# A macaron block (feed-forward, attention, feed-forward): VectorE's small operations in another order, transposes in other PSUM banks, zero filling by GpSimd

## The chip, the core and the metric

The kernel runs on one core of a Trainium2 chip. A core has five engines with a queue each: TensorE (PE), VectorE (DVE), ScalarE (ACT), GpSimd (POOL) and SyncE (SP), the last used for DMA. They run on their own and wait for each other by semaphores. The metric is the device time of one execution in microseconds. Before the change it is 1791.26 us, the median of three runs (1790.68 to 1792.49).

## The reference

```
x = x + 0.5 * ffn(layernorm(x))
x = x + attention(layernorm(x))
x = x + 0.5 * ffn(layernorm(x))

def ffn(x):                       # x: 4 batches x 1024 tokens x 128
    weights = routing(x)          # tokens x 8 experts
    gate = x @ Wg[e];  up = x @ Wu[e]          # 8 experts, 128 x 128 each
    h = silu(gate) * up
    return sum over e of weights[:, e] * (h @ Wd[e])

def routing(x):                   # per token, over the 8 experts
    inh = sigmoid(x @ Wr / temperature)
    w = exp(-|inh - 1/e| / 0.1) where inh lies in a zone, else 0
    where no expert is in the zone: the two best of exp(-|inh - 1/e| / 0.3), normalized
    return w / sum(w)
```

The attention has 16 heads of 64 with rotary positions and its own layernorm with scale and bias; the change does not touch it. Input and output are float32 arrays of 4096 x 128.

## The kernel before

The program is three blocks one after the other: `ffn("f1")`, the attention, `ffn("f2")`. The names f1 and f2 stand for the two feed-forwards below.

A feed-forward makes four turns, t = 0 to 3, one for each batch of 1024 tokens. A turn has 16 units, k = 0 to 15: units 0 to 7 are the eight experts on the first 512 tokens, units 8 to 15 the same experts on the other 512. The running number of a unit is i = 16 t + k. The work of one unit goes through the engines in this order:

- PE, `gate_up` (L481 to L483 twice): three f16 products of 128x512 for the gate into PSUM bank 0 or 1, then three for up into bank 2 or 3. The banks alternate from unit to unit.
- ACT, `silu` (L574): the gate bank to `gate`.
- POOL (L623): `gate` times the token's routing weight, which a DMA has spread over the partitions (`w_all`, a ring of 4), to `gw`.
- DVE (L754): `gw` times the up bank to `hw`. This is called the product of a unit here.
- PE, `down` (L497): four float32 products that add the unit to y in bank 6 (units 0 to 7) or bank 7 (units 8 to 15).
- DVE, `add_y` (L706): y times 0.5 is added to x, once for each bank and turn.

PE's queue in a turn is gate_up(k + 2), down(k), gate_up(k + 3), down(k + 1) and so on. So PE is two units ahead with gate and up. The up products of unit k + 2 wait for the product of unit k (`s_hw`), because they take the same PSUM bank; POOL's L623 of unit k + 2 waits for it too, because it takes the same half of `gw`.

Between the units of a turn the next batch is made ready:

- `norm` on DVE (L283 to L307): the layernorm's mean and inverse root for batch t + 2, 27 small steps, most of them on 128x8 elements, each waiting for the one before it. Its last step (L307) releases ACT's `normed` (L545) at units 0 and 1 of the next turn.
- `transpose` on PE (L448), two halves; `hi` on ACT (L550) and `lo` on DVE (L638) split the result into two f16 parts.
- `router` on PE (L457, 24 small products), `logits` on DVE (L642), `tanh_z` and `tanh_dist` on ACT (L554 to L564), and then `route` on DVE (L664 to L698), 28 parts of which 26 are operations on 128x64 or 128x8 elements.
- `weight_rows` on PE (L470) and `rows` on ACT (L568): the routing weights transposed, then out to memory and back by SP's DMAs as the rows that POOL reads.
- In f1 only: a second `norm`, of 43 steps, for the attention's layernorm of batch t - 1, and POOL's and ACT's `up_low` and `up_high` (L228, L223).

The order of DVE's queue is written out by hand in `turn(t, last)`: the lists `between[k]` and `after_[k]` say which steps stand before and behind the product of unit k. In the last turn of f1 DVE also fills areas for the attention (`clear`, L328 and L334: nine fills of 128x1024 elements and four of 1x1024).

Of the kernel before, what the change touches and what calls it, by code (L numbers as in the profile page):

```python
# [60 lines left out]
def build(nc, x, wg, wu, wd, wr, temp, wdq, wdkv, wup_in, wuv, wo, lns, lnb, rope, out):  # L61
    with ExitStack() as ctx:
# [297 lines left out]
        def ffn(name):  # L360
# [36 lines left out]
            with nc.Block() as block:  # L397
# [41 lines left out]
                def _(pe):  # L439
                    def transpose(p, a):  # L440
# [4 lines left out]
                        elif p > 0:  # L445
                            pe.wait_ge(s_y, 2 * p - 1)
                        for j in range(4):
                            last = nc.tensor.transpose(ps[:, 7, P * j:P * j + P], xn[:, a, j, :], ident[:])  # L448
                        last.then_inc(s_xT, 1)

                    def router(p):

                        pe.wait_ge(s_xlo, 2 * p + 2)
                        for j in range(TB):
                            cols = bass.ds(p * S + P * j, P)
                            for k, (a, b) in enumerate(((xt_hi, wr_hi), (xt_hi, wr_lo), (xt_lo, wr_hi))):
                                last = nc.tensor.matmul(ps[:, 7, E * j:E * j + E], a[:, cols], b[:],  # L457
# [43 lines left out]
                    def turn(t, last):  # L501
                        for k in range(16):
# [32 lines left out]
                def _(act):  # L535
# [12 lines left out]
                    def hi(p, a):  # L548
                        act.wait_ge(s_xT, 2 * p + (a + 1))
                        nc.scalar.copy(xt_hi[:, bass.ds(p * S + 512 * a, 512)], ps[:, 7, :]).then_inc(s_xhi, 1)  # L550
# [15 lines left out]
                    def rows(p, a):  # L566
                        act.wait_ge(s_wr, 2 * p + (a + 1))
                        nc.scalar.copy(w_rows[0:E, p % 2, a, :], ps[0:E, 6, :]).then_inc(s_wt, 1)  # L568
# [7 lines left out]
                    def turn(t, last):  # L576
                        for k in range(16):
# [37 lines left out]
                def _(pool):  # L615
# [11 lines left out]
                    if first:  # L627
                        identities(pool)
                    if first:
# [679 lines left out]
```

## Time and profile before

| | |
|---|---|
| time, median of 3 | 1791.26 us (1790.68 to 1792.49) |
| time of the profiled execution | 1791.68 us |
| its span | 1789.9 us |
| PE busy | 1652.9 us, 92% |
| DVE busy | 1508.4 us, 84% |
| ACT busy | 1238.2 us, 69% |
| POOL busy | 1316.2 us, 74% |
| TensorE clock granted, mean | 0.973 of full speed |
| f1, first to last add_y | 46.2 to 217.7 us |
| f2, to its last add_y | 1786.5 us |

The span is the time from the first to the last instruction that the profiler recorded. Busy shares are averages over three blocks with different limits, so what a change in a feed-forward is worth is read inside f1 and f2. In a timeline, each row is one instruction or some alike behind one another; the number in brackets at its end is how long the engine stood idle before it, and for whom. The duration of an instruction that waits for a resource, and not for a semaphore, contains that wait.

### The profile page before, as it was taken

To read this page: it belongs to the slowest core of one execution; us is meant where nothing else is said; L and a number is where in the kernel's file an instruction comes from. 1 tells how busy PE (TensorE), PEld (TensorE's weight loads), DVE (VectorE), ACT (ScalarE), POOL (GpSimd) and SP (SyncE) were. 2 spreads that over 40 slices of the span, in tenths; PEclk is the share of its full clock that TensorE was granted. 3 is DMA by queue.
4 is the path that set the end of the run, shared out by engine and by line. 5 is a ranking of instruction groups with operands and counts; after the bars stand their busy time and mean duration, and the time that the engine had idled before them with its cause. 6 is when DMAs were issued, how large, how long until landed. Compare 5 with 4: busy or idle time off the path is not lost. (4 is left out here: it accounts for less than half of the span.)

```text
span 1789.9 us, 48884 instructions
## 1 busy us (share of the span) xinstructions
PE 1652.9 (92%) x19376; PEld 1062.1 (59%) x19376; DVE 1508.4 (84%) x3091; ACT 1238.2 (69%) x1747; POOL 1316.2 (74%) x922
## 2 busy tenths in 40 slices
PE   3999766999999999999999999999999999966999
PEld 2666532666666666666666666666666666644666
DVE  4888897999999999999999999999999999856763
ACT  3343353888888888888888888887888888863332
POOL 1455424888888888888888888888888888752545
PEclk9899877999999999999999999999999999997999
DMA  6233203111111122111111112211111111102334
GB/s 196 92 103 104 59 1 71 37 37 37 37 38 37 41 51 55 37 38 37 37 37 37 37 39 50 55 41 38 37 37 37 37 38 37 37 2 78 119 108 125
DMA packets 65346, 97.22 MB, mean 54 GB/s; under 512 B 11488, under 2 KB 23776, under 8 KB 64864
## 3 DMA queue, kind: packets, MB, share of 16 engines
q1 hardware_dynamic: 62320, 93.23, 20.0%
q8 instruction: 156, 2.56, 0.6%
q10 hardware_dynamic: 2800, 0.85, 0.2%
q14 instruction: 70, 0.57, 0.1%
HBM read 41.23 MB, written 2.36 MB: 24 GB/s over the span
## 5 line engine op out<-in xcount | busy, mean ns | idle before, releaser
L1214 POOL TENSOR_TENSOR area<-area 128x1024 f16<-128x1024 f32 (+1 forms) x512 | 833.0, 1645 | 159.8 <-ACT area L1182 137.7
L1108 DVE TENSOR_REDUCE area<-ps 128x1 f32<-128x512 f32 x1024 | 668.7, 685 | 60.1 <-PE ps L988 52.3
L1180 ACT ACTIVATE area<-ps 128x1024 f16<-128x1024 f32 x512 | 524.6, 1025 | 233.8 <-PE ps L1015 232.9
L1034 PE MATMUL ps<-cv_all,area 128*128 128x64 f16 x4096 | 458.9, 195 | 0.0
L1032 PE MATMUL ps<-cv_all,area 128*128 128x65 f16 x4096 | 457.0, 193 | 1.5 <-POOL area L1214 1.5
L1036 PE MATMUL ps<-cv_all,area 128*128 128x65 f16 x4096 | 455.6, 193 | 0.0
L1034 PEld LDWEIGHTS ps<-cv_all,area 128*128 128x128 f16 x4096 | 381.2, 97 | 86.2
L1032 PEld LDWEIGHTS ps<-cv_all,area 128*128 128x128 f16 x4096 | 384.0, 97 | 51.7 <-POOL area L1214 1.4
L1014 PE MATMUL ps<-area 128*128 128x512 f16 x1024 | 390.5, 381 | 18.5 <-DVE area L1132 17.7
L988 PE MATMUL ps<-area 128*128 128x512 f16 x1024 | 394.5, 386 | 8.6 <-DMA area<-area 5.4
L1015 PE MATMUL ps<-area 128*128 128x512 f16 x1024 | 389.2, 380 | 0.0
L1036 PEld LDWEIGHTS ps<-cv_all,area 128*128 128x128 f16 x4096 | 382.9, 99 | 0.0
L623 POOL TENSOR_TENSOR area<-area 128x512 f32<-128x512 f32 x128 | 162.1, 1270 | 206.7 <-ACT area L574 120.3
L1182 ACT ACTIVATE area<-ps 128x1024 f32<-128x1024 f32 x256 | 261.4, 1021 | 0.0
L1104 DVE TENSOR_TENSOR area<-ps,cs 128x512 f32<-128x512 f32 x256 | 175.8, 688 | 54.4 <-PE ps L982 54.0
L1222 POOL TENSOR_TENSOR area<-area 128x512 f32<-128x512 f32 x128 | 163.0, 1273 | 46.0 <-DVE area L1104 40.3
L1132 DVE TENSOR_TENSOR area<-ps,area 128x512 f16<-128x512 f32 x256 | 174.2, 680 | 12.8 <-ACT ps L1186 12.8
L574 ACT ACTIVATE area<-ps 128x512 f32<-128x512 f32 x128 | 75.5, 594 | 143.5 <-PE ps L483 133.5
L1014 PEld LDWEIGHTS ps<-area 128*128 128x128 f16 x1024 | 99.6, 97 | 114.3 <-DVE area L1132 81.6
L988 PEld LDWEIGHTS ps<-area 128*128 128x128 f16 x1024 | 99.2, 97 | 114.2 <-DVE area L1108 32.8
L754 DVE TENSOR_TENSOR area<-area,ps 128x512 f32<-128x512 f32 x128 | 87.1, 681 | 88.4 <-POOL area L623 82.6
L1186 ACT ACTIVATE ps<-ps 128x512 f32<-128x512 f32 x256 | 155.5, 607 | 0.0
(161 smaller groups left out, 2433.3 us busy)
## 6 DMA issues: line engine op xcount, KB each, us to landing
area<-area SPq DMA_DIRECT2D x384, 128.0 KB, 2.3
area<-f_w_rows_in_dram SPq DMA_DIRECT2D x128, 256.0 KB, 3.3
xg<-in_x SPq DMA_DIRECT2D x4, 512.0 KB, 7.2
area<-in_wup SPq DMA_DIRECT2D x1, 2048.0 KB, 10.4
out_x<-xg SPq DMA_DIRECT2D x3, 512.0 KB, 4.9
cs<-in_rope SPq DMA_DIRECT2D x1, 1024.0 KB, 11.1
area<-area SPq DMA_DIRECT2D x64, 2.0 KB
area<-in_wo ACTq DMA_DIRECT2D x1, 512.0 KB, 6.7
```

The lines of the kernel that those rows point to most:

```text
L988: last = nc.tensor.matmul(bank, qk["Q1"][:, slot, hd, P * qt:P * qt + P], qk["K1"][:, slot, hd, 512 * kh:512 * kh + 512], start=True, stop ...
L1014: nc.tensor.matmul(o, qk["K1"][:, k, hd, keys], qk["Q1"][:, k, hd, qs], start=True, stop=False)
L1015: return nc.tensor.matmul(o, qk["K2"][:, k, hd, keys], qk["Q2"][:, k, hd, qs], start=False, stop=True)
L1032: nc.tensor.matmul(o, p_hi[:, s % 4, c:c + P], latents[:, 0:DH + 1], start=first, stop=False, skip_group_check=True)
L1034: nc.tensor.matmul(o[:, 0:DH], p_hi[:, s % 4, c:c + P], latents[:, DH + 1:CV], start=False, stop=False, skip_group_check=True)
L1036: last = nc.tensor.matmul(o, p_lo[:, s % 4, c:c + P], latents[:, 0:DH + 1], start=False, stop=(kt == 7), skip_group_check=True)
L1104: nc.vector.tensor_tensor((ra, rb)[sw][:, c % 2, :], bank, cs[:, sw, 512 * half_:512 * half_ + 512], ALU.mult).then_inc(s_mr, 1)
L1108: nc.vector.tensor_reduce(mx[:, hd, kh, qt:qt + 1], bank, AX.X, ALU.max).then_inc(s_mr, 1)
L1132: nc.vector.tensor_tensor(p_lo[:, s % 4, 0:512], ps[:, 2, :], p_hi[:, s % 4, 0:512], ALU.subtract).then_inc(s_pd, 1)
L1180: nc.scalar.activation(p_hi[:, s % 4, :], sc, ACT.Exp, scale=0.125).then_inc(s_e16, 1)
L1182: nc.scalar.activation(p32_even[:, (s // 2) % 2, :], sc, ACT.Exp, scale=0.125).then_inc(s_e32, 1)
L1214: nc.gpsimd.tensor_tensor(p_lo[:, s % 4, c0:], src[:, (s // 2) % 2, :], p_hi[:, s % 4, c0:], ALU.subtract).then_inc(s_pp, 1)
```

## The change

In the feed-forward's code:

- The transposes and the router's result go to PSUM bank 5 and the weight rows to bank 4. They had been in banks 7 and 6, which y also uses. The waits follow: `down` at unit 0 and at unit 8 now waits for `add_y` alone.
- The second transpose moves from unit 3 to unit 4, ACT's second `hi` from unit 4 to unit 5, and the router from unit 5 to unit 6.
- On DVE, `lo` stands behind the products of units 3 and 5, no longer ahead of them. `add_y` of bank 6 moves from unit 9 to unit 11. `route` has 7 parts behind each of the units 7 to 10 (8, 8, 8 and 4 before).
- `norm` for batch t + 2 had stood behind units 2 to 5 and 11 to 13. Now it has 4 and 2 steps behind units 0 and 1, then 2, 1, 8 and 10 behind units 12, 13, 14 and 15.
- In f1, the attention's `norm` had 3 steps behind every unit from 1 on, alternating with the others. Now it has 4, 2, 6, 3 and 6 steps behind units 2 to 6 and 4, 6, 7 and 5 behind units 11 to 14, in one piece each.
- The 13 fills of `clear` leave DVE's last turn in f1 and stand in POOL's queue at the start of the program, ahead of `low_halves`.

```diff
-        def clear(v, n):
+        def clear(pool, n):
 
             if n > 8:
-                v.wait_ge(s_qz, 8)
-                nc.vector.memset(qk["K2"][64:65, (n - 9) // 2, (n - 9) % 2, :], -MAX_SCALE).then_inc(s_qz, 1)
+                pool.wait_ge(s_qz, n)
+                nc.gpsimd.memset(qk["K2"][64:65, (n - 9) // 2, (n - 9) % 2, :], -MAX_SCALE).then_inc(s_qz, 1)
                 return
...
-            nc.vector.memset(t_, 0.0).then_inc(s_qz, 1)
+            nc.gpsimd.memset(t_, 0.0).then_inc(s_qz, 1)
...
                         elif p > 0:
-                            pe.wait_ge(s_y, 2 * p - 1)
+                            pe.wait_ge(s_zr, p)
                         for j in range(4):
-                            last = nc.tensor.transpose(ps[:, 7, P * j:P * j + P], xn[:, a, j, :], ident[:])
+                            last = nc.tensor.transpose(ps[:, 5, P * j:P * j + P], xn[:, a, j, :], ident[:])
...
                             if p > 0:
-                                pe.wait_ge(s_y, 2 * p)
+                                pe.wait_ge(s_wt, 2 * p)
...
-                            last = nc.tensor.transpose(ps[0:E, 6, P * j:P * j + P], w[:, 4 * a + j, :], ident[:])
+                            last = nc.tensor.transpose(ps[0:E, 4, P * j:P * j + P], w[:, 4 * a + j, :], ident[:])
...
-                        if k == 0:
-                            pe.wait_ge(s_wt, 2 * t + 2)
+                        if k == 0 and t > 0:
+                            pe.wait_ge(s_y, 2 * t)
                         if k == E:
-                            if last_turn:
-                                pe.wait_ge(s_y, 2 * t + 1)
-                            else:
-                                pe.wait_ge(s_zr, t + 2)
+                            pe.wait_ge(s_y, 2 * t + 1)
...
-                            if not last and k == 5:
+                            if not last and k == 6:
                                 router(t + 1)
                             down(i, t, k, last)
-                            if not last and k in (1, 3):
-                                transpose(t + 1, (k - 1) // 2)
+                            if not last and k in (1, 4):
+                                transpose(t + 1, k // 4)
...
-                                if k in (2, 4):
-                                    hi(t + 1, (k - 2) // 2)
+                                if k in (2, 5):
+                                    hi(t + 1, k // 5)
...
                         identities(pool)
+                        for n in range(13):
+                            clear(pool, n)
+                        pool.wait_ge(s_qz, 13)
...
+                        def put(parts, counts):
+                            for k, count in counts.items():
+                                for _ in range(count):
+                                    after_[k].append(parts.pop(0))
+                            assert not parts, len(parts)
                         after_[1].append(lambda: add_y(t, 1))
-                        after_[9].append(lambda: add_y(t, 0))
+                        after_[11].append(lambda: add_y(t, 0))
                         if not last:
-                            between[3].append(lambda: lo(t + 1, 0))
-                            between[5].append(lambda: lo(t + 1, 1))
+                            after_[3].append(lambda: lo(t + 1, 0))
+                            after_[5].append(lambda: lo(t + 1, 1))
                             after_[6].append(lambda: logits(t + 1))
-                            for parts, n_between, n_after in (
-                                    (norm(v, t + 3, s_ch, s_rstd), {}, {2: 5, 3: 5, 4: 5, 5: 5, 11: 4, 12: 4, 13: 4}),
-                                    (route(t + 1), {}, {k: 8 for k in range(7, 11)})):
...
+                            put(route(t + 1), {k: 7 for k in range(7, 11)})
                         if first:
                             parts = norm(v, t + 0, s_an, s_ann, True)
                             parts[0] = lambda stats=parts[0]: (v.wait_ge(s_y, 2 * t + 1), stats())
-                            for k in range(1, 16):
-                                mine, others = [parts.pop(0) for _ in range(min(3, len(parts)))], after_[k]
...
+                            put(parts, {2: 4, 3: 2, 4: 6, 5: 3, 6: 6, 11: 4, 12: 6, 13: 7, 14: 5})
                         if first and last:
                             for k in range(4):
-                                after_[9 + k].append(lambda k=k: down_low(v, k))
-                            for k in range(13):
-                                after_[2 + k].append(lambda k=k: clear(v, k))
+                                after_[7 + k].append(lambda k=k: down_low(v, k))
+                        if not last:
+                            put(norm(v, t + 3, s_ch, s_rstd), {0: 4, 1: 2, 12: 2, 13: 1, 14: 8, 15: 10})
```

The changed file is 16 lines shorter, so lines behind the diff's places have other numbers there: L754 is L738, L574 is L571, L497 is L494, L623 is L620.

ScalarE's queue over units 2 to 9 of a turn of f1; a turn of f2 has the same order here, without L223. L574 (L571 after) is `silu`, L550 (L547) is `hi`, L554 to L564 (L551 to L561) are the tanh steps. Before:

```order
L550 CAST xt_hi<-ps 128x512
L574 ACTIVATE area<-ps 128x512 x2
L550 CAST xt_hi<-ps 128x512
L574 ACTIVATE area<-ps 128x512 x2
L554 ACTIVATE area<-area 128x64
L561 ACTIVATE area<-area,tanh_bias 128x64 x2
L564 ACTIVATE area<-area 128x128
L574 ACTIVATE area<-ps 128x512 x3
```

After:

```order
L547 CAST xt_hi<-ps 128x512
L571 ACTIVATE area<-ps 128x512 x3
L547 CAST xt_hi<-ps 128x512
L571 ACTIVATE area<-ps 128x512
L551 ACTIVATE area<-area 128x64
L558 ACTIVATE area<-area,tanh_bias 128x64 x2
L561 ACTIVATE area<-area 128x128
L571 ACTIVATE area<-ps 128x512 x3
```

The second `hi` has moved behind one more `silu`. The tanh steps keep their place, behind the `silu` of unit 7 and ahead of that of unit 8, while the router that feeds them stands one unit later on PE (`k == 5` and `k == 6` in the diff).

DVE's queue from the product of unit 8 on, in a turn of f2, where L664 to L698 are route. Before:

```order
L754 TENSOR_TENSOR area<-area,ps 128x512
L673 SCALAR_TENSOR_TENSOR area<-area 128x64
L674 TENSOR_TENSOR area<-area,rev 128x64
L675 TENSOR_REDUCE area<-area 128x8
L676 TENSOR_REDUCE area<-area 128x8
L677 TENSOR_SCALAR area<-area 128x8
L678 TENSOR_TENSOR area<-area 128x64
L679 SCALAR_TENSOR_TENSOR area<-area 128x64
L680 TENSOR_REDUCE area<-area 128x8
L754 TENSOR_TENSOR area<-area,ps 128x512
L706 SCALAR_TENSOR_TENSOR xg<-ps,xg 128x512
L681 TENSOR_TENSOR area<-area 128x64
```

After:

```order
L738 TENSOR_TENSOR area<-area,ps 128x512
L672 TENSOR_TENSOR area<-area 128x64
L673 SCALAR_TENSOR_TENSOR area<-area 128x64
L674 TENSOR_TENSOR area<-area,rev 128x64
L675 TENSOR_REDUCE area<-area 128x8
L676 TENSOR_REDUCE area<-area 128x8
L677 TENSOR_SCALAR area<-area 128x8
L678 TENSOR_TENSOR area<-area 128x64
L738 TENSOR_TENSOR area<-area,ps 128x512
L679 SCALAR_TENSOR_TENSOR area<-area 128x64
L680 TENSOR_REDUCE area<-area 128x8
L681 TENSOR_TENSOR area<-area 128x64
```

Seven parts of route stand between two products in place of eight, and `add_y` (L706) is no longer behind the product of unit 9.

DVE's queue at the end of a turn of f2, from the product of unit 14 to that of the next turn's unit 1. L754 (L738 after) is the product of a unit. Before, five products follow one another, with nothing between them, up to `add_y`:

```order
L307 SCALAR_TENSOR_TENSOR minus_mean_rstd<-mean,rstd 128x8
L754 TENSOR_TENSOR area<-area,ps 128x512 x5
L706 SCALAR_TENSOR_TENSOR xg<-ps,xg 128x512
```

After, the same place reads:

```order
L738 TENSOR_TENSOR area<-area,ps 128x512
L248 TENSOR_TENSOR root_tmp<-rstd 128x8
L249 TENSOR_TENSOR root_tmp<-root_tmp,minus_half_var 128x8
L250 SCALAR_TENSOR_TENSOR rstd<-root_tmp,rstd 128x8
L248 TENSOR_TENSOR root_tmp<-rstd 128x8
L249 TENSOR_TENSOR root_tmp<-root_tmp,minus_half_var 128x8
L250 SCALAR_TENSOR_TENSOR rstd<-root_tmp,rstd 128x8
L248 TENSOR_TENSOR root_tmp<-rstd 128x8
L249 TENSOR_TENSOR root_tmp<-root_tmp,minus_half_var 128x8
L250 SCALAR_TENSOR_TENSOR rstd<-root_tmp,rstd 128x8
L307 SCALAR_TENSOR_TENSOR minus_mean_rstd<-mean,rstd 128x8
L738 TENSOR_TENSOR area<-area,ps 128x512
```

These ten steps stand between the product of unit 15 and that of the next unit 0. Eight more, L286 to L246, stand between those of units 14 and 15.

## Rows read from the trace of the kernel before

**Rows 1.** windows of turns: PE, PEld, DVE, ACT, POOL busy; clock, DMA, GB/s

```profile
69.95:113.00 43.05, 39.42 (x264) 27.75 (x264) 36.74 (x120) 16.68 (x33) 22.57 (x18) 0.96 0.33 99
...
1695.80:1735.20 39.40, 37.84 (x265) 26.80 (x264) 27.28 (x75) 15.74 (x32) 20.27 (x17) 1.00 0.39 121
```

**Rows 2.** timeline of PE, f2 (start us, us; wait in brackets)

```profile
1691.24 0.38 PE L481 MATMUL ps<-xt_hi,wg_hi 128*128 128x512 f16 x1
...
1693.43 0.38 PE L481 MATMUL ps<-xt_hi,wg_hi 128*128 128x512 f16 x1
...
1699.91 0.39 PE L481 MATMUL ps<-xt_hi,wu_hi 128*128 128x512 f16 x1 [1.30 <-DVE area L754]
```

**Rows 3.** chain that ended last, f2 (start us, us, what)

```profile
1687.64 0.59 PE ps L457 x24
...
1703.81 0.45 PE ps L470 x4
```

**Rows 4.** timeline of ACT, second turn of f2

```profile
1688.58 0.26 ACT L554 ACTIVATE area<-area 128x64 f32<-128x64 f32 x1 [0.96 <-DVE area L642]
...
1689.90 0.60 ACT L574 ACTIVATE area<-ps 128x512 f32<-128x512 f32 x1
```

**Rows 5.** timeline of POOL, second turn of f2

```profile
1690.58 1.27 POOL L623 TENSOR_TENSOR area<-area 128x512 f32<-128x512 f32 x1 [1.60 <-ACT area L574]
...
1692.76 1.27 POOL L623 TENSOR_TENSOR area<-area 128x512 f32<-128x512 f32 x1 [0.91 <-ACT area L574]
...
1700.03 1.30 POOL L623 TENSOR_TENSOR area<-area 128x512 f32<-128x512 f32 x1 [1.62 <-DVE area L754]
```

**Rows 6.** timeline of DVE, second turn of f2, units 7 to 12

```profile
1690.57 0.95 DVE L665 RECIPROCAL area<-area 128x128 f32<-128x128 f32 x1
...
1692.44 0.68 DVE L754 TENSOR_TENSOR area<-area,ps 128x512 f32<-128x512 f32 x1
...
1693.04 1.07 DVE L673 SCALAR_TENSOR_TENSOR area<-area 128x64 f32<-128x64 f32 x1
...
1697.29 1.19 DVE L685 TENSOR_TENSOR area<-area 128x64 f32<-128x64 f32 x1
...
1699.18 0.68 DVE L754 TENSOR_TENSOR area<-area,ps 128x512 f32<-128x512 f32 x1
...
1701.33 0.67 DVE L754 TENSOR_TENSOR area<-area,ps 128x512 f32<-128x512 f32 x1
...
1702.11 0.17 DVE L249 TENSOR_TENSOR root_tmp<-root_tmp,minus_half_var 128x8 f32<-128x8 f32 x1
...
1702.31 0.17 DVE L250 SCALAR_TENSOR_TENSOR rstd<-root_tmp,rstd 128x8 f32<-128x8 f32 x1
```

**Rows 7.** timeline of DVE, second turn of f2, units 14 and 15

```profile
1709.34 0.69 DVE L754 TENSOR_TENSOR area<-area,ps 128x512 f32<-128x512 f32 x1 [1.93 <-POOL area L623]
...
1710.57 0.69 DVE L754 TENSOR_TENSOR area<-area,ps 128x512 f32<-128x512 f32 x1 [0.54 <-POOL area L623]
```

**Rows 8.** timeline of PE, first turn of f1

```profile
75.00 0.61 PE L481 MATMUL ps<-xt_hi,wu_hi 128*128 128x512 f16 x1 [2.55 <-DVE area L754]
```

**Rows 9.** windows of f1 around it

```profile
75.00:78.00 3.00, 3.00 (x12) 2.35 (x13) 3.00 (x15) 0.00 (x0) 1.29 (x1) 0.52 0.00 0
```

**Rows 10.** timeline of DVE, f1: first turn's end, then the last turn

```profile
87.97 1.23 DVE L306 TENSOR_SCALAR rstd_plus<-rstd 128x8 f32<-128x8 f32 x1
...
176.15 0.69 DVE L754 TENSOR_TENSOR area<-area,ps 128x512 f32<-128x512 f32 x1 [1.21 <-POOL area L623]
...
200.63 0.91 DVE L334 MEMSET area<- 128x1024 f32 x1 [0.16 <-issue]
...
214.13 0.69 DVE L754 TENSOR_TENSOR area<-area,ps 128x512 f32<-128x512 f32 x1
```

**Rows 11.** timeline of POOL, start of the program

```profile
0.73 0.20 POOL L178 MEMSET ident<- 128x128 f32 x1 [0.29 <-POOLq L1299]
...
17.28 0.20 POOL L175 TENSOR_TENSOR wr_lo<-area,wr_hi 128x8 f16<-128x8 f32 x1 [14.75 <-ACT wr_hi L168]
```

More of the change, by code:

```diff
@@ L456, in router @@
                             for k, (a, b) in enumerate(((xt_hi, wr_hi), (xt_hi, wr_lo), (xt_lo, wr_hi))):
-                                last = nc.tensor.matmul(ps[:, 7, E * j:E * j + E], a[:, cols], b[:],
+                                last = nc.tensor.matmul(ps[:, 5, E * j:E * j + E], a[:, cols], b[:],
                                                         start=(j == 0 and k == 0), stop=(k == 2), skip_group_check=True)
@@ L549, in hi @@
                         act.wait_ge(s_xT, 2 * p + (a + 1))
-                        nc.scalar.copy(xt_hi[:, bass.ds(p * S + 512 * a, 512)], ps[:, 7, :]).then_inc(s_xhi, 1)
+                        nc.scalar.copy(xt_hi[:, bass.ds(p * S + 512 * a, 512)], ps[:, 5, :]).then_inc(s_xhi, 1)
                     def tanh_z(p):
@@ L567, in rows @@
                         act.wait_ge(s_wr, 2 * p + (a + 1))
-                        nc.scalar.copy(w_rows[0:E, p % 2, a, :], ps[0:E, 6, :]).then_inc(s_wt, 1)
+                        nc.scalar.copy(w_rows[0:E, p % 2, a, :], ps[0:E, 4, :]).then_inc(s_wt, 1)
                     def silu(i, t, k):
@@ L708, in turn @@
                     def turn(t, last):
-                        spread = [0] * 16
-                        between, after_ = ({k: [] for k in range(16)} for _ in range(2))
+                        after_ = {k: [] for k in range(16)}
+                        def put(parts, counts):
[3 more added lines that the diff above has]
+                            assert not parts, len(parts)
                         after_[1].append(lambda: add_y(t, 1))
-                        after_[9].append(lambda: add_y(t, 0))
+                        after_[11].append(lambda: add_y(t, 0))
                         if not last:
-                            between[3].append(lambda: lo(t + 1, 0))
-                            between[5].append(lambda: lo(t + 1, 1))
+                            after_[3].append(lambda: lo(t + 1, 0))
+                            after_[5].append(lambda: lo(t + 1, 1))
                             after_[6].append(lambda: logits(t + 1))
-                            for parts, n_between, n_after in (
-                                    (norm(v, t + 3, s_ch, s_rstd), {}, {2: 5, 3: 5, 4: 5, 5: 5, 11: 4, 12: 4, 13: 4}),
-                                    (route(t + 1), {}, {k: 8 for k in range(7, 11)})):
-                                for k in range(16):
-                                    for part_list, count in ((between, n_between), (after_, n_after)):
-                                        for _ in range(count.get(k, 0)):
-                                            if parts:
-                                                part_list[k].append(parts.pop(0))
-                                assert not parts, len(parts)
+                            put(route(t + 1), {k: 7 for k in range(7, 11)})
                         if first:
@@ L731, in turn @@
                             parts[0] = lambda stats=parts[0]: (v.wait_ge(s_y, 2 * t + 1), stats())
-                            for k in range(1, 16):
-                                mine, others = [parts.pop(0) for _ in range(min(3, len(parts)))], after_[k]
-                                after_[k] = []
-                                if k == 1:
-                                    after_[k].append(others.pop(0))
-                                while mine or others:
-                                    for some in (others, mine):
-                                        if some:
-                                            after_[k].append(some.pop(0))
-                            assert not parts
+                            put(parts, {2: 4, 3: 2, 4: 6, 5: 3, 6: 6, 11: 4, 12: 6, 13: 7, 14: 5})
                         if first and last:
                             for k in range(4):
-                                after_[9 + k].append(lambda k=k: down_low(v, k))
-                            for k in range(13):
-                                after_[2 + k].append(lambda k=k: clear(v, k))
+                                after_[7 + k].append(lambda k=k: down_low(v, k))
+                        if not last:
+                            put(norm(v, t + 3, s_ch, s_rstd), {0: 4, 1: 2, 12: 2, 13: 1, 14: 8, 15: 10})
                         for k in range(16):
                             i, b = t * 16 + k, k % 2
-                            for f in between[k]:
-                                f()
                             v.wait_ge(s_gw, i + 1)
```

4 lines of the change are left out of this document (2 added, 2 removed).

## The prediction

> **What bounds the kernel now.** I read the windows first, a turn of a feed-forward each, from one add_y to the same one of the next turn. A turn of f1 takes 43.05 us, one of f2 39.40 us [rows 1]. PE is busy for 37.8 us of the latter. Then the timeline of PE: with nothing to wait for, a unit comes every 2.19 us (gate products at 1691.24 and 1693.43) [rows 2]. Sixteen units are 35.0 us; the router adds 0.6 and four groups of transposes 0.45 each [rows 3]. So PE alone needs about 37.4 us a turn. A turn of f2 loses 2.0 us on top, one of f1 5.7. Six such turns and the last turn of f1 hold everything that the change can win: 3 x 2.0 + 3 x 5.7 = 23.1 us, and what the last turn loses, 7.4 us. (The product of unit 1 starts at 176.15 and that of unit 15 at 214.13 [rows 10], 38.0 us for 14 units that PE makes in 30.6.)
>
> Who makes PE wait? Always DVE's product L754: 1.30 us at 1699.91 in f2 [rows 2], 2.55 us at 75.00 in f1, after which the matmul itself takes 0.61 us in place of 0.38 [rows 8], and the three microseconds from there have a granted clock of 0.52, the lower level of 1.2 GHz [rows 9]. DVE is late because of its small operations, and their cost is not what their size says. L673 takes 1.07 us at 1693.04 and L685 1.19 us at 1697.29, while L249 and L250 of the same kinds take 0.17 [rows 6]. POOL's L623 runs from 1692.76 for 1.27 us [rows 5], and L673 ends just behind it. So a small operation of DVE that meets L623 waits until L623 ends. L306, a TENSOR_SCALAR with one input, does the same in f1, 1.23 us [rows 10]. The product L754 reads PSUM and takes 0.68 us in all these rows, inside such a stretch or not.
>
> By the Trainium skill ("SBUF — State Buffer", section Who interferes with whom), VectorE and GpSimd share a port pair that one instruction holds to its end; VectorE needs it for two SBUF inputs, if the GpSimd instruction reads SBUF, and for its two-port modes. This trace agrees, at 1.07 to 1.23 us a time.
>
> This is the rule that I work with: when DVE is late, POOL's next L623 is released by the product itself. L754 starts at 1699.18 for 0.68 us, L623 at 1700.03 [rows 5, 6], 0.17 us behind its end. Then it holds up the small operations for 1.27 us. A list of n chained steps behind a late product costs 0.7 + 0.2 + 1.3 us and 0.2 us for each step that did not slip in ahead (L249 and L250 start 0.20 us apart [rows 6]). That passes PE's 2.19 us as soon as any step is left over.
>
> **The change, part by part, on the turn of f2 that the rows show.**
>
> *Router one unit later.* PE gives it behind gate_up of unit 8: 2.19 us later. ACT's queue is in order, and the tanh steps stand ahead of silu of unit 8. Before, they start at 1688.58 and that silu at 1689.90 without any idle time [rows 4]. Now the silu starts at 1692.09, POOL's L623 of unit 8 at 1692.77 (1690.58 + 2.19 [rows 5]), and that of unit 9 right behind, 1694.04 to 1695.31, since its silu is ready. DVE starts route at about 1692.1: L664 0.25, L665 0.95 [rows 6], L666 waits to 1694.04, L671 to 1695.31. The product of unit 8 starts at 1695.4; before, it was at 1692.44 [rows 6]. PE wants it for 1694.08 (1693.43 + 0.65 of gate): PE stands 2.0 us.
>
> *Route in sevens.* Now DVE is late, and the products of units 9, 10 and 11 follow by the rule. The shared part is 0.7 + 0.2 + 1.3 = 2.2 us. Behind unit 8 one step waits and four short ones follow, most of them unchained at 0.13: 2.85 us. Behind unit 9 four chained ones of 0.25 follow: 3.25 us. Behind unit 10 five to six: 3.5 us. That of unit 11 starts at 1705.0 and not at 1701.33 [rows 6]. There PE had no slack before (up of unit 13 at 1702.11 was due within 0.1 us of it), so the turn is 3.6 us longer. Moving add_y away takes 0.6 us out of this stretch, which is counted; before, the wait for POOL at unit 9 ran under it and cost nothing.
>
> *Norm at units 14 and 15.* Before, the products of 14 and 15 start at 1709.34 and 1710.57 [rows 7]; DVE is idle for 1.93 us ahead of the first, as POOL comes late, and PE takes the result at once, so from here every microsecond that DVE adds beyond PE's pace is PE's. Eight steps behind unit 14 now meet what is left of L623 of unit 15 (0.6) and that of the next unit 0 (1.1): 0.6 + 0.6 + 1.2 + 1.1 = 3.5 us. Ten behind unit 15: 0.6 + 0.4 for two steps + 1.25 + 8 x 0.2 = 3.85 us. Against two units of PE, 7.35 - 4.4 = 2.9 us. ACT's normed waits for the last step; its own 1.6 us and the silu behind it are covered by PE's two units ahead.
>
> Sum for a turn of f2: 3.6 + 2.9 = 6.5 us, three turns 19.5 us.
>
> *A turn of f1* has the same route stretch, 5.1 us of PE's waits (the 1.5 that f2 has there before, 1.30 of it in one row [rows 2], plus 3.6). To it come 0.9 us behind unit 5, where lo now waits for ACT and three steps follow it into L623, and about 1.0 us because POOL's L228 stands directly behind L623 of unit 11 and holds DVE once more: 7.0 us. At the end of the turn the lists have 8, 13 and 10 steps behind units 13, 14 and 15: 4.7 us (L228 and two L623 are met), 3.85 and 3.8 us, against 6.6 us of PE: 5.8 us. 37.4 + 7.0 + 5.8 = 50.2 us against 43.1: 7.1 us a turn, three turns 21.3 us. What is won in it, the 43 steps taken out of units 7 to 10, is in that balance.
>
> *The last turn of f1* loses the 13 fills, 0.91 us for a big one [rows 10]. It has no route. Its lists of 6, 6, 7 and 5 still pass PE's pace: I get 0.8 us lost behind unit 6, 1.8, 1.1 and 1.0 behind 12, 13 and 14, together 4.7 us against 7.4: 2.7 us won.
>
> *Fills on POOL.* A POOL fill of 128 elements takes 0.20 us, and POOL is idle for 14.75 us ahead of its L175 at 17.28 [rows 11]. Nine fills of 1024 elements and four more are at least 13 x 0.9 us (DVE's rate [rows 10]), which the idle time hides; at eight times 0.20 they are 21 us, and 6 us late for the router's low half. They may also hold DVE's TENSOR_SCALAR steps in the first norm. I take 1 us, near the lower end, since the 0.20 us has a fixed part; bounds 0 and 6.
>
> By the same section of the Trainium skill a GpSimd instruction that only writes does not stop a VectorE instruction with two inputs, so the fills would hold up TENSOR_SCALAR alone. No row here shows it.
>
> *PSUM banks.* The waits that go (down of unit 0 on the weight rows, down of unit 8 on the logits) do not show as idle time of PE in any row that I read: nothing.
>
> Sum: 19.5 + 21.3 - 2.7 + 1 = 39.1 us. The profiled execution took 1791.7 us, which gives 1830.8; the median of the runs is 0.4 lower, and 1830 us is the round figure.
>
> **Rivals.**
> - *The even deal works* (faster). If steps slip in between POOL's operations, a list of 10 costs 0.7 + 2.0 us and turns fall to about 38.3 us: 3 x 4.8 + 3 x 1.1 + 5 won, 1769 us. For it: counted by the steps' own lengths without POOL, route's four lists and their products come to 8.9 us against PE's 4 x 2.19 = 8.76. Against it: every list of f1 that the rows touch holds one long step. It decides if the products of units 14, 15 and 0 stay under 2.2 us apart. 0.11.
> - *Only the router's move costs* and the ends of turns are free: 3 x 3.6 + 3 x 1.2 - 2.7 + 1 = 12.7, 1804 us. The idle time of 1.93 us ahead of unit 14 [rows 7] speaks for it. 0.16.
> - *The clock falls as well.* PE's waits of 2 us and more bring what the 2.55 us brought at 75.00 [rows 8], in six turns, 2 us each where DVE does not hide it: 1842 us. 0.13.
> - *No effect*: f1's gain in units 7 to 10 pays for all: 0.04.
>
> **The numbers.** The forecast, by which a late DVE meets POOL in nearly every list, has 0.56. Within 0.2% (3.6 us, about what a measurement of this kernel can tell from no change) 0.04; faster 0.12; slower 0.84. The range of 1796 to 1848 leaves out the faster cases and little above. Each length above rests on who wins the race for a free moment, which I estimate at 0.3 us a list (one chained step of route); over some 40 such lists that is 12 us either way.
>
> **What would show it.** Right: a turn of f2 of 46 us and of f1 of 50; PE's waits for L738 at units 10 to 13 and at the next turn's units 0 to 2; silu of unit 8 directly behind the tanh steps with gate long done; a step of 1.2 us in each of the lists behind units 14 and 15. Wrong: products of units 14, 15 and 0 about 2.2 us apart, or PE busy for 37 of 38 us in a turn.

## The result, and the profile after

The changed kernel takes 1814.72 us (median of 4 runs, 1813.60 to 1816.29), the kernel before 1790.97 us in runs beside them: a ratio of 1.0132, 95% interval 1.0117 to 1.0147. It is slower by 23.7 us. The prediction said 1830 us, range 1796 to 1848.

The profiled execution spans 1813.6 us at a mean clock of 0.974 (before 1789.9 and 0.973), so the clock is no part of it. The windows below are a turn of f1 and one of f2, from the product of unit 0 to the next one, with the columns of [rows 1].

```profile
97.67:144.74 47.07, 40.47 (x264) 26.79 (x264) 39.06 (x119) 16.36 (x33) 22.49 (x18) 0.96 0.29 92
1689.28:1732.94 43.66, 38.67 (x264) 26.44 (x264) 28.62 (x75) 15.43 (x32) 20.29 (x16) 1.00 0.36 110
```

A turn of f2 went from about 39.6 to 43.7 us, one of f1 from about 43.2 to 47.1; 46 and 50 were forecast. The timeline of DVE after, in units 7 to 11 of that turn of f2 (start, us, what; in brackets the idle time ahead and who ended it), answers to [rows 6]:

```profile
1707.03 0.23 DVE L664 TENSOR_SCALAR area<-area 128x128 f32<-128x128 f32 x1 [0.69 <-ACT area L561]
...
1709.14 0.98 DVE L671 SCALAR_TENSOR_TENSOR area<-area 128x64 f32<-128x64 f32 x1
1710.05 0.68 DVE L738 TENSOR_TENSOR area<-area,ps 128x512 f32<-128x512 f32 x1
1710.65 0.21 DVE L672 TENSOR_TENSOR area<-area 128x64 f32<-128x64 f32 x1
...
1711.31 0.97 DVE L677 TENSOR_SCALAR area<-area 128x8 f32<-128x8 f32 x1
1712.20 0.21 DVE L678 TENSOR_TENSOR area<-area 128x64 f32<-128x64 f32 x1
1712.33 0.68 DVE L738 TENSOR_TENSOR area<-area,ps 128x512 f32<-128x512 f32 x1
...
1714.21 0.99 DVE L685 TENSOR_TENSOR area<-area 128x64 f32<-128x64 f32 x1
1715.12 0.67 DVE L738 TENSOR_TENSOR area<-area,ps 128x512 f32<-128x512 f32 x1
...
1716.22 1.26 DVE L690 TENSOR_TENSOR area<-area 128x64 f32<-128x64 f32 x1
...
1718.36 0.68 DVE L738 TENSOR_TENSOR area<-area,ps 128x512 f32<-128x512 f32 x1
```

Each list holds one step of about 1 us. POOL and ACT of the same stretch, against [rows 4, 5], show why, and what the router's later unit does:

```profile
1707.56 2.49 POOL L620 TENSOR_TENSOR area<-area 128x512 f32<-128x512 f32 x2 [3.57 <-ACT area L571]
1710.89 1.36 POOL L620 TENSOR_TENSOR area<-area 128x512 f32<-128x512 f32 x1 [0.85 <-DVE area L738]
```

```profile
1705.78 0.26 ACT L551 ACTIVATE area<-area 128x64 f32<-128x64 f32 x1 [3.14 <-DVE area L642]
...
1706.90 1.07 ACT L571 ACTIVATE area<-ps 128x512 f32<-128x512 f32 x2
```

Two silus come back to back behind the tanh steps, two of POOL's operations behind them, and the small step of DVE ahead of the product of unit 8 (L671) ends with the second: 1707.56 + 2.49 is 1710.05. The long step L677 ends at 1712.28, the POOL operation from 1710.89 at 1712.25. PE pays, where it had waited once in [rows 2], after the products of units 8, 10 and 11:

```profile
1710.78 0.39 PE L481 MATMUL ps<-xt_hi,wu_hi 128*128 128x512 f16 x1 [1.53 <-DVE area L738]
1715.85 0.39 PE L481 MATMUL ps<-xt_hi,wu_hi 128*128 128x512 f16 x1 [0.43 <-DVE area L738]
1719.09 0.39 PE L481 MATMUL ps<-xt_hi,wu_hi 128*128 128x512 f16 x1 [0.88 <-DVE area L738]
```

The lists behind units 14 and 15, against [rows 7]:

```profile
1682.51 0.69 DVE L738 TENSOR_TENSOR area<-area,ps 128x512 f32<-128x512 f32 x1 [1.85 <-POOL area L620]
1683.11 0.62 DVE L286 TENSOR_TENSOR mean_dif<-stat 128x8 f32<-128x8 f32 x1
...
1684.38 1.27 DVE L245 TENSOR_SCALAR rstd<-var_eps 128x8 int32<-128x8 int32 x1
...
1685.79 0.69 DVE L738 TENSOR_TENSOR area<-area,ps 128x512 f32<-128x512 f32 x1
...
1686.79 1.14 DVE L250 SCALAR_TENSOR_TENSOR rstd<-root_tmp,rstd 128x8 f32<-128x8 f32 x1
...
1689.28 0.69 DVE L738 TENSOR_TENSOR area<-area,ps 128x512 f32<-128x512 f32 x1
```

And the start of the program, where POOL was idle in [rows 11] and now fills (POOL, then DVE):

```profile
2.37 8.23 POOL L334 MEMSET area<- 128x1024 f16 x9
10.66 3.95 POOL L328 MEMSET area<- 1x1024 f16 x4
```

```profile
7.54 0.17 DVE L286 TENSOR_TENSOR mean_dif<-stat 128x8 f32<-128x8 f32 x1
...
7.82 0.97 DVE L289 TENSOR_SCALAR mean<-mean_sum 128x8 f32<-128x8 f32 x1
...
9.74 0.88 DVE L245 TENSOR_SCALAR rstd<-var_eps 128x8 int32<-128x8 int32 x1
10.66 0.97 DVE L246 TENSOR_SCALAR minus_half_var<-var_eps 128x8 f32<-128x8 f32 x1
11.67 0.17 DVE L248 TENSOR_TENSOR root_tmp<-rstd 128x8 f32<-128x8 f32 x1
```

Beside the fills a step with two inputs takes 0.17 us (L286, L248), while each TENSOR_SCALAR within SBUF ends as a fill of POOL ends: L289 at 8.79, L245 at 10.62, where the ninth fill ends at 10.60. One step with two inputs, L290 at 7.94, shows 0.86 us, but it stands behind L289 in DVE's queue and ends 0.01 us after it.

**The ledger.** From the starts of the products in the profiled executions, in us. "Start" is the first product; a turn runs from unit 0's product to the next one; the last turn of f1 ends with the start of its last add_y.

| kernel | median | start | f1, 3 turns | f1, last turn | f2, 3 turns |
|---|---|---|---|---|---|
| before | 1790.97 | 44.65 | 129.60 | 42.73 | 119.21 |
| after | 1814.72 | 48.24 | 143.48 | 36.24 | 132.99 |
| e1 fills on POOL | 1787.85 | 48.17 | 129.79 | 35.74 | 120.02 |
| e2 router back | 1803.86 | 48.60 | 135.56 | 36.24 | 128.51 |
| e3 norm back | 1809.33 | 46.74 | 137.90 | 37.81 | 128.89 |
| e4 reductions | 1802.80 | 43.45 | 139.90 | 36.23 | 126.98 |
| e5 before, small in PSUM | 1767.27 | 43.66 | 114.98 | 36.93 | 114.06 |
| e6 after, small in PSUM | 1775.57 | 44.62 | 122.98 | 33.28 | 118.01 |
| e7 e5 and fills on POOL | 1764.94 | 44.13 | 114.89 | 34.30 | 115.26 |
| e8 router later alone | 1812.83 | 43.66 | 137.80 | 42.48 | 132.10 |
| e9 banks alone | 1791.92 | 44.83 | 129.81 | 42.60 | 119.48 |
| e10 norm alone | 1801.88 | 44.84 | 135.97 | 40.65 | 126.75 |
| e11 banks and route | 1783.69 | 43.70 | 121.75 | 41.44 | 120.58 |
| e12 attention norm alone | 1804.01 | 44.44 | 139.85 | 44.23 | 120.17 |

After less before: start +3.6, f1's turns +13.9, its last turn -6.5, f2's turns +13.8; the attention -0.1 and f2's last turn -1.2 (34.48 to 33.28) make the sum +23.5.

### The profile page after: what moved, and what is told of

Read it like the earlier page. It is cut to its first block and busy times, and to the rows that moved or that the text cites. A ratio compares the mean times of both kernels' runs of the same rounds, so it can differ in the third digit from the quotient of the medians.

```text
span 1813.6 us, 48882 instructions
## 1 busy us (share of the span) xinstructions
PE 1658.5 (91%) x19376; PEld 1059.4 (58%) x19376; DVE 1513.1 (83%) x3078; ACT 1236.8 (68%) x1747; POOL 1328.9 (73%) x935
## 5 line engine op out<-in xcount | busy, mean ns | idle before, releaser
L620 POOL TENSOR_TENSOR area<-area 128x512 f32<-128x512 f32 x128 | 162.2, 1273 | 229.9 <-ACT area L571 145.8
L1116 DVE TENSOR_TENSOR area<-ps,area 128x512 f16<-128x512 f32 x256 | 174.4, 681 | 12.8 <-ACT ps L1170 12.8
L571 ACT ACTIVATE area<-ps 128x512 f32<-128x512 f32 x128 | 74.6, 592 | 149.1 <-PE ps L483 139.9
L738 DVE TENSOR_TENSOR area<-area,ps 128x512 f32<-128x512 f32 x128 | 87.3, 683 | 89.0 <-POOL area L620 85.3
```

Of the source, the lines that this page charges most:

```text
L620: nc.gpsimd.tensor_tensor(gw[:, k % 2, :], gate[:, k % 2, :], w_all[:, i % RING, :], ALU.mult).then_inc(s_gw, 1)
```

## The experiments

The edits are shown in short form, with names cut and lines drawn together.

**e1, the fills alone.** The kernel before, with

```diff
+ for n in range(13): clear(pool, n)      # behind identities(pool)
- for k in range(13): after_[2 + k].append(lambda k=k: clear(v, k))
```

> The kernel before, with the 13 fills moved from DVE's last turn of f1 to the head of POOL's queue, and nothing else. Port theory: the fills hold up DVE's TENSOR_SCALAR steps of the first norm, five steps of about 0.9 us in place of 0.17, so the first product starts at 48.2 us and not at 44.65 (+3.6); the last turn of f1 gets 5 to 7 us shorter; about 1788 us in all. Rival, that POOL's idle time hides the fills: first product at 44.7, 1785 us. Rival, that the 3.6 us at the start come from another part of the change: first product at 44.7.

Measured 1787.85, ratio 0.9984 (0.9974 to 0.9993). The fills do both things at once: start +3.5, last turn -7.0.

**e2 and e3, parts undone in the changed kernel.** e2 puts the router in unit 5 again, the transposes in 1 and 3, hi in 2 and 4; e3 the norm:

```diff
- if not last and k == 6:      router(t + 1)
+ if not last and k == 5:      router(t + 1)
- put(norm(...), {0: 4, 1: 2, 12: 2, 13: 1, 14: 8, 15: 10})
+ put(norm(...), {2: 5, 3: 5, 4: 5, 5: 5, 11: 4, 12: 3})
```

> The changed kernel with the router, the second transpose and the second hi back in their old units (5, 3 and 4); DVE's lists stay as changed. If the router's move costs: the products of units 5 to 7 come 2.2 us closer together and silu of unit 8 no longer stands behind the tanh steps, 2 us a turn in six turns, about 1802 us. Rival, that DVE's own lists set the pace there and the router's place is nothing: 1814 us, unchanged within 2 us.

> The changed kernel with norm for batch t + 2 back behind units 2 to 5, 11 and 12 (5, 5, 5, 5, 4, 3 steps); all else as changed. If the lists behind units 14 and 15 cost 3.3 us a turn: products 14, 15 and 0 are 1.2 and 2.0 us apart again in f2, six turns give back 2 to 3 us each (part of it is paid again in units 2 to 5), about 1799 us. Rival, that the 18 steps cost their length wherever they stand: 1814 us.

e2 gave 1803.86 (1.0067, 1.0050 to 1.0083), 10.9 us back, near the 1802 that was expected. e3 gave 1809.33 (1.0104, 1.0089 to 1.0120), 5.4 us back where 16 were expected: the end of a turn of f2 won 3.4 us (unit 13 to the next unit 0, 9.22 to 5.79) and units 0 to 7 gave 2.4 of it back.

**e4, the same number of steps, but of a kind that should not wait.** The changed kernel with the norm's chained steps as TENSOR_REDUCE of one input, chain and order kept; it leaves out the inverse root.

```diff
- made = [lambda: nc.vector.tensor_tensor(ms, m_e, m_o, ALU.add), ...]
+ made = [lambda o=o, a=a: nc.vector.tensor_reduce(o, a.unsqueeze(2), AX.X, ALU.add) for o, a in steps]
```

> The changed kernel with the 18 steps behind the statistics and the last step of norm for batch t + 2 replaced by reductions of the same shape with one input, in the same units and the same chain of waits; the inverse root is left out by that. Port theory: none of them waits for POOL any more, so in f2 product 15 follows 14 after 2.2 us (3.12 now) and product 0 follows 15 after 2.6 to 2.7 us (3.48 now); 1.7 us a turn in f2 and 1 to 2 us in f1, 1804 to 1808 us. Rival, that only the number and the chain of the steps count: 3.1 and 3.5 us as now, 1814 us.

Measured 1802.80 (1.0064, 1.0049 to 1.0079), 11.9 us less. The list behind unit 15, chained reductions, half of them beside a POOL operation that runs from 1678.01 to 1679.28:

```profile
1677.73 0.69 DVE L748 TENSOR_TENSOR area<-area,ps 128x512 f32<-128x512 f32 x1
1678.34 0.15 DVE L285 TENSOR_REDUCE root_tmp<-rstd 128x8 f32<-128x8 f32 x1
1678.53 0.16 DVE L285 TENSOR_REDUCE root_tmp<-root_tmp 128x8 f32<-128x8 f32 x1
...
1680.20 0.69 DVE L748 TENSOR_TENSOR area<-area,ps 128x512 f32<-128x512 f32 x1
```

2.47 us in place of 3.5, nothing held. The start won 4.8 us as well, which the expectation had left out. So the hold is real, and the rest (ten steps at 0.2 us) is the list's own length.

**e5 and e6, operands in PSUM.** e4 leaves work out. A way to keep the work and lose the hold: in each two-input step one input in a free PSUM bank, the other in SBUF, and the source or the result of each one-input step in PSUM. e5 is this on the kernel before, e6 on the changed one. (Steps such as the square of one tensor are written as a product with the other factor first; the norm has one step more.)

```diff
- tt(t0, fb_all, wide(r2), ALU.is_equal)            # all in SBUF
+ tt(t0_p, fb_all, wide(r2), ALU.is_equal)          # t0_p and fb_all in PSUM
- tensor_tensor(tmp, root, root); tensor_tensor(tmp, tmp, minus_half)
+ tensor_tensor(tmp, minus_half, root); tensor_tensor(tmp, tmp, root)   # root in SBUF
```

> The kernel before, its order untouched, but each small step of route and of the norms has one of its operands (or the result of a one-input step) in PSUM banks 4 and 5, which the feed-forwards leave unused; the norm has one step more. Theory (a small step of DVE with two inputs in SBUF, or a TENSOR_SCALAR within SBUF, waits for POOL's L623 to end): no small step takes over 0.4 us any more, f2's turns fall from 39.6 to about 38 us, f1's from 43.2 to about 39, its last turn loses some 4 us less, together 1791 - 5 - 12 - 4 = about 1770 us. Rival (the chain of semaphore waits is what costs, POOL or not, and operands in PSUM are slower to reach): the steps take 0.2 to 0.3 us each, the turns keep their length, 1791 or more.

> The kernel after with its lists as they are and the small steps' operands in PSUM bank 4 in the same way (weight rows in bank 5 with the transposes). Theory: the lists of eight and ten behind units 14 and 15 cost 0.7 + 0.2 for each step, 2.3 and 2.9 us, and not 3.1 and 3.5; route's sevens fit in 2.2 us; f2's turns fall from 43.7 to about 39, f1's from 47.1 to about 40.5, 1815 - 14 - 20 = about 1781 us. If the hold by POOL were the whole of what made the changed order slow, it would equal the kernel before in PSUM; what is left above that is the order's own price. Rival (the number of steps in a list decides, not POOL): 1810 or more.

e5 took 1767.27 us (0.9864, 0.9848 to 0.9880), e6 1775.57 us (0.9911, 0.9897 to 0.9926): 24 us less than the kernel before and 39 us less than the changed one, both within 6 us of the figures expected (1770 and 1781). The timeline of DVE in e5, units 8 and 9 of f2, and of POOL beside it:

```profile
1668.69 0.68 DVE L772 TENSOR_TENSOR area<-area,ps 128x512 f32<-128x512 f32 x1
1669.29 0.21 DVE L691 SCALAR_TENSOR_TENSOR area<-area,ps 128x64 f32<-128x64 f32 x1
1669.42 0.21 DVE L692 TENSOR_TENSOR area<-ps,rev 128x64 f32<-128x64 f32 x1
...
1669.80 0.16 DVE L695 TENSOR_SCALAR area<-ps 128x8 f32<-128x8 f32 x1
...
1670.67 0.69 DVE L772 TENSOR_TENSOR area<-area,ps 128x512 f32<-128x512 f32 x1
```

```profile
1669.37 1.27 POOL L641 TENSOR_TENSOR area<-area 128x512 f32<-128x512 f32 x1 [0.92 <-ACT area L592]
...
1671.55 1.27 POOL L641 TENSOR_TENSOR area<-area 128x512 f32<-128x512 f32 x1 [0.92 <-ACT area L592]
```

L691 to L695 run beside POOL's L641 at their own length. L691 is the step that took 1.07 us as L673 in [rows 6]. POOL is released by ACT here and not by DVE, so DVE is no longer late. A turn of either feed-forward is PE's alone (us, then PE's busy time first):

```profile
82.30:120.56 38.26, 38.00 (x267) 27.07 (x266) 27.48 (x122) 16.95 (x34) 22.46 (x18) 1.00 0.37 116
1649.64:1687.87 38.23, 37.96 (x267) 27.07 (x266) 23.10 (x76) 16.00 (x33) 20.26 (x16) 1.00 0.42 127
```

The Trainium skill ("SBUF — State Buffer", Who interferes with whom) says that a VectorE instruction with at most one SBUF input and outside the two-port modes does not contend with GpSimd; these rows agree, at 0.16 to 0.21 us a step.

e6 stays 8.3 us above e5. That is what the changed order costs with the hold gone: of the 23.7 us, some two thirds need the hold, and a third (the list behind unit 15 still takes 2.76 us) does not.

The hold did not become much more frequent by the change. Of DVE's steps on 128x64 elements or fewer, 39 took over 0.4 us in the three turns of f1 before and 36 after, 15 and 21 in the three of f2. What these took above 0.2 us each is 28.9 and 29.4 us in f1, 12.8 and 17.2 us in f2: 4.9 us more, for turns that are 27.7 us longer. By this count most of the loss is holds and lists that now stand where DVE has no time to spare, and not added holds. In e5 one such step is left in these six turns, in e6 none, and DVE has time to spare (27.48 us busy of 38.26).

**e7, both together.** e5 with e1's fills.

> The kernel before with the small steps' operands in PSUM and the 13 fills at the head of POOL's queue. The fills alone started the first turn 3.5 us later, since they held the TENSOR_SCALAR steps of the first norm, and gave 7 us in the last turn of f1. Theory (the hold needs operands in SBUF): with results in PSUM the first norm isn't held, the first product comes at about 45 us, and the time is 3 to 5 us below the same kernel with the fills on DVE. Rival (the fills delay POOL's low halves and so the start): first product at 48 us, the same time within 2 us.

1764.94 us (0.9853, 0.9835 to 0.9870), the fastest kernel of all. The first product comes at 44.13, so the start is as before the fills moved; the last turn gave 2.6 us. The median is 2.3 us below e5, a little under what was expected: without the hold the fills on DVE had cost less.

**e8, the router alone.** The kernel before, with

```diff
- router at k == 5, transposes at 1, 3, hi at 2, 4, between[5]: lo(t + 1, 1)
+ router at k == 6, transposes at 1, 4, hi at 2, 5, after_[5]: lo(t + 1, 1)
```

> The kernel before with the router, the second group of transposes and its high half one unit later, and the second low half behind the product of unit 5 in place of ahead of it; lists and banks as before. Theory of the prediction (silu of unit 8 stands behind the tanh steps, PE stands 2.0 us and DVE is late from there): 3 to 3.6 us a turn, 1791 + 6 x 3.3 = 1811 us. By what putting it back gave in the changed kernel (1.8 us a turn of f2, 2.5 of f1, 10.9 us in all) it is 1802. Rival (it costs only together with lists of seven): under 1795.

1812.83 us (1.0119, 1.0101 to 1.0137): 21 us, nearly the whole loss, with one part. In the second turn of f2 the products of units 4 and 8 are 14.37 us apart and were 10.36; from unit 8 to 13 nothing changes (14.30 and 14.28). Of these 4.0 us half, 2.0, lies between units 4 and 6, where lo now stands behind the product of unit 5 and waits for ACT's hi with the norm's steps behind it:

```profile
1695.80 0.69 DVE L754 TENSOR_TENSOR area<-area,ps 128x512 f32<-128x512 f32 x1
1698.45 0.69 DVE L638 TENSOR_TENSOR xt_lo<-ps,xt_hi 128x512 f16<-128x512 f32 x1 [1.97 <-ACT xt_hi L550]
...
1699.26 1.19 DVE L246 TENSOR_SCALAR minus_half_var<-var_eps 128x8 f32<-128x8 f32 x1
...
1700.99 0.69 DVE L754 TENSOR_TENSOR area<-area,ps 128x512 f32<-128x512 f32 x1
```

5.19 us between two products. In the changed kernel the norm has left unit 5, and the same two are 3.41 apart; from unit 4 to 6 it is then 5.60 us, against 5.48 before and 7.45 in e8. The other half lies between units 6 and 8 (4.87 to 6.92 us; 7.43 in the changed kernel): the tanh steps start at 1703.50, two silus and two of POOL's operations follow back to back, as in the changed kernel.

**e9 to e12, the other parts alone**, each on the kernel before:

```diff
e9:  transposes and logits in bank 5, weight rows in bank 4, their waits as in the changed kernel
e10: {2: 5, 3: 5, 4: 5, 5: 5, 11: 4, 12: 4, 13: 4} -> {0: 4, 1: 2, 12: 2, 13: 1, 14: 8, 15: 10}
e11: e9, and route {k: 8} -> {k: 7}, add_y(t, 0) from after_[9] to after_[11]
e12: attention norm {1..15: 3 each, interleaved} -> {2: 4, 3: 2, 4: 6, 5: 3, 6: 6, 11: 4, 12: 6, 13: 7, 14: 5}
```

> The kernel before with the changed PSUM banks and their waits alone: transposes and logits in bank 5, weight rows in bank 4. Theory of the prediction: PE waited at none of the waits that go, so 1791 us, within 2 us of the kernel before. Rival (down of unit 0 or of unit 8 was held up by the weight rows or the logits, and the transposes by add_y): 3 us or more faster.

> The kernel before with the steps of the norm for the next but one turn in the changed units alone (4, 2, 2, 1, 8 and 10 behind units 0, 1, 12, 13, 14 and 15). Theory of the prediction: the products of units 14 and 15 come 7.4 us and not 4.4 us apart in two steps, 2.9 us a turn, nothing comes back: 1791 + 17 = 1808 us. By the changed trace they come 3.3 us later, but units 2 to 5, now free of these steps, give up to 1.1 us back (the norm put back cost that much there), 2.2 us a turn: 1804. Rival, from what putting it back gave (5.4 us in all): 1796.

> The kernel before with the changed banks, route in sevens and add_y of the first half behind unit 11 in place of unit 9; the router stays in its unit. Theory: with the router in its unit DVE enters unit 7 on time, and route's lists of seven cost at most what add_y's move leaves: the wait for POOL ran under add_y at unit 9 and now stands in the open, up to 1 us a turn: 1791 + 6 = 1797 us. Rival (shorter lists are cheaper): 3 us or more faster than the banks alone.

> The kernel before with the attention norm's steps in f1 in the changed units (4, 2, 6, 3, 6 behind units 2 to 6; 4, 6, 7, 5 behind 11 to 14) and none in 7 to 10; all else as before. f2 must not change. Units 7 to 10 of a turn of f1 lose 2.4 us more than in f2 and can give that back (7 us in three turns). Theory (a late list costs 2.2 us and 0.2 for each step): units 2 to 6 and 11 to 14 take all of it back and more, 1791 to 1796 us. Rival: the even deal pays, 1785 us or less.

- e9: ratio 1.0006 (0.9998 to 1.0015). By themselves the banks are worth nothing that can be told from no change.
- e10: 1.0068 (1.0055 to 1.0081), 12 us. The figure with the relief of units 2 to 5 in it (1804) was near.
- e11: 0.9962 (0.9950 to 0.9974), 6.8 us faster; the rival wins, but in f1 alone. f1's three turns fall by 7.9 us: its units 8 to 10 from 11.33 to 9.66 us (2.67, 3.36 and 3.63) in each, and units 11 and 12 from 6.5 and 6.8 to 5.4 us in the first two, which ran at a mean clock of 0.90 and 0.96 before and of 0.94 and 1.00 here. f2's three turns are 1.4 us longer. Which of the two moves, the sevens or add_y, does it was not run apart.
- e12: 1.0070 (1.0056 to 1.0084), 12.5 us slower; both theories miss.

What e12 did: with no second chain between them, its steps follow each other at 0.20 us. DVE in e12, behind a product of f1:

```profile
122.99 0.15 DVE L248 TENSOR_TENSOR root_tmp<-rstd 128x8 f32<-128x8 f32 x1
123.18 0.17 DVE L249 TENSOR_TENSOR root_tmp<-root_tmp,minus_half_var 128x8 f32<-128x8 f32 x1
123.38 0.17 DVE L250 SCALAR_TENSOR_TENSOR rstd<-root_tmp,rstd 128x8 f32<-128x8 f32 x1
```

In the kernel before the attention norm alternates with the other norm (and with route), and two steps fit in that time:

```profile
77.50 0.17 DVE L249 TENSOR_TENSOR root_tmp<-root_tmp,minus_half_var 128x8 f32<-128x8 f32 x1
77.58 0.17 DVE L248 TENSOR_TENSOR root_tmp<-rstd 128x8 f32<-128x8 f32 x1
77.70 0.17 DVE L250 SCALAR_TENSOR_TENSOR rstd<-root_tmp,rstd 128x8 f32<-128x8 f32 x1
```

0.08 and 0.12 us apart. Holds are not what e12 adds: 33 steps over 0.4 us in the three turns of f1, against 39. But the clock is a second cause. The third turn of f1 before and in e12, and three microseconds of the latter (columns of [rows 1]):

```profile
132.38:174.25 41.87, 38.18 (x266) 26.63 (x264) 36.48 (x119) 16.64 (x34) 22.59 (x18) 1.00 0.37 101
137.10:184.29 47.19, 41.44 (x266) 27.95 (x265) 38.48 (x118) 16.59 (x33) 22.48 (x18) 0.93 0.28 90
170.10:173.10 3.00, 3.00 (x10) 1.53 (x9) 2.69 (x15) 0.00 (x0) 0.00 (x0) 0.52 0.00 0
```

PE waited 2.68 us for DVE's product up to 168.29, and the granted clock is 0.52, the lower level of 1.2 GHz, from 170.10 to 173.10; PE is busy for 3.3 us more in that turn with the same matmuls. The four turns of f1 have a mean clock of 0.91, 0.94, 0.93 and 0.91 in e12, of 0.90, 0.96, 1.00 and 1.00 before and of 0.91, 0.96, 1.00 and 1.00 in the changed kernel. How e12's 12.5 us divide between the spacing of the steps and the clock no run shows.

**Parts and whole.** Alone: router 21.3, norm 12.2, attention norm 12.5, banks and route -6.8, fills -2.9, together 36.3 us by the ratios, against 23.7 for the whole. They overlap, and by the ledger most of it in f2: its three turns add up to 23.6 us by the parts and to 13.8 in the whole, those of f1 to 17.1 and 13.9. (Fills and attention norm, which leave f2 as it is, have 1.8 of the 23.6, so that much is scatter between profiled executions.) In the second turn of f2, units 4 to 8 account for the larger half: the parts add 3.9 us there and the whole 2.7, since the norm's move takes away the steps that made the router's move dear in unit 5. Units 8 to 10 give the rest (0.4 us more by the parts, 0.6 less in the whole). So the price of a part depends on what stands beside it: the router's move is 10.9 us by its undo (e2) and 21.3 alone (e8), the norm's 5.4 (e3) and 12.2 (e10).

## Why the prediction was right, and where it was off

The sign, the mechanism and most of the places were right; the sum was 16 us too high (39.1 against 23.5), more than the 12 us that the prediction gave its races, and the time lies in the range since the range is wide. Turns of f2 were priced 5.7 us too high, those of f1 7.4, the last turn of f1 3.8; the start, 2.6 too low, hid some of it.

- *A small step waits for POOL's operation.* Right, shown by e4 (the same steps as reductions: no hold), e5 and e6 (24 and 39 us). It was the bound of the kernel before too: 24 us lay in it, as much as the change lost.
- *Router one unit later, PE stands 2.0 us.* Right in kind: silu behind the tanh steps, PE waits [1.53] at 1710.78. Product 8 comes 2.7 us later relative to unit 4 (10.36 to 13.04 us), 3.0 forecast.
- *Route in sevens: 2.85, 3.25 and 3.5 us.* This step failed in size: 2.28, 2.79 and 3.24, together 1.3 us less. In the first, five steps slipped in at 0.13 us apart before the held one; the hold came late in the first two and was cut to 0.97 and 0.99 us; only the third had a full one (1.26). Router and route are +2.1 us a turn of f2, not 3.6. Without the router's move the sevens and add_y's move are a gain in f1 and 0.5 us a turn of loss in f2 (e11).
- *Norm at units 14 and 15: +2.9.* Measured +3.3 (5.90 to 9.22 us from unit 13 to the next unit 0), each list with its step of 1.1 to 1.3 us. What was left out is what the norm's old places give back: from unit 0 to unit 4 it is 1.35 us less (9.08 to 7.73; with the norm moved alone, e10, 7.74). The prediction has no term for it in any turn. 2.1 + 3.3 - 1.35 is 4.05 for the turn for which 6.5 was forecast.
- *f1: +7.1 a turn.* Measured +4.9, +3.9 and +5.1. The end was nearly as worked out (units 13 to 15 take 11.67 us; 12.35 forecast). The middle, units 0 to 12, takes 35.4 us where 37.85 was forecast: units 8 to 10 take 8.63 and not 9.6, the 1.0 us for L228 behind unit 11 does not show (5.36 us from unit 11 to 13, as in f2), and units 0 to 3 have 1.4 us less than before. Only the 0.9 us behind unit 5 came true (4.50 us to the next product, 3.41 in f2). That the 43 steps cost 0.20 us each in one piece and about 0.1 us interleaved was not in the working.
- *Last turn of f1: -2.7.* -6.5. The fills alone give 7.0 (e1).
- *Fills on POOL: +1, bounds 0 and 6.* +3.5. The sentence that held (they may hold the TENSOR_SCALAR steps of the first norm) was priced too low: four TENSOR_SCALARs of 0.9 to 1.0 us nearly in a row, for 0.2.
- *PSUM banks: nothing.* Right (e9).
- *Rivals.* The clock did not fall: 0.974, the turn of f1 at 0.96 as in [rows 1]. "Only the router's move costs" (1804) falls with e10 (12 us without it); yet the router's move alone is the dearest part. "The even deal works" falls with the products of units 14, 15 and 0, 3.12 and 3.48 us apart and not 2.2.

Open: what the parts cost in pairs, which would say how their 36 us fold into 24; how much of e12 is the clock; and whether e11's lists on top of e7 would go lower still. None of it was run.

## What to carry to other kernels

Where VectorE and GpSimd run side by side, count a small VectorE step as 0.2 us if at most one of its inputs is in SBUF, or, for a TENSOR_SCALAR, if its source or its result is in PSUM; a reduction of one input was not held either (e4). Else price it by what is left of GpSimd's operation. Two free PSUM banks for small intermediates were worth 24 us here, more than any order of the steps that was tried. By the rows of f1, two chains of dependent steps interleaved take hardly longer than one. When a list of steps is moved, credit the place that it leaves. A part measured alone and the same part undone can differ twofold, so neither is "the" price of it.

## What was not expected of the hardware

- One-input TENSOR_SCALARs on 128x8 float32 wait for a GpSimd fill, 0.86 to 0.97 us against 0.17, while two-input steps beside the same fills take 0.17 unless they are queued behind a held one. With its source in PSUM (e7) such a step took 0.17 us beside the fills. The Trainium skill ("VectorE: DVE Perf Modes", Why PSUM operands drop a tier) gives the reason that a PSUM operand rules out the mode with both SBUF ports; the rows agree, and show that the wait comes even with eight elements a partition.
- A GpSimd fill of one partition takes as long as one of 128: 3.95 us for four against 8.23 us for nine.
- A small step that is not held is no slower for an operand in PSUM: 0.17 us at 128x8 and 0.21 to 0.23 us at 128x64 in both places.
